# One recurrence step: gates and tanh of the cell held in PSUM, and the input gate activated on its own

## The reference, cut to what matters

```
def step(carry, xs):
    h, c = carry
    i_t = sigmoid(xi_t + h @ V_i)
    g_t = tanh(xg_t + h @ V_c)
    o_t = sigmoid(xo_t + h @ V_o)
    c_new = h * c + i_t * g_t
    h_new = o_t * tanh(c_new)
```

## Time and profile before

| | |
|---|---|
| median of three runs | 982.26 us |
| the profiled execution, its own time | 980.65 us |
| its span, first to last instruction | 978.9 us |
| mean granted TensorE clock | 0.755 of full speed |
| busy in the span: PE, DVE, ACT, POOL | 768.5, 552.2, 554.3, 369.5 us |
| first and last start of L470 | 145.7 us, 567.3 us |

### The profile page before, as it was taken

The page is one execution under the profiler, slowest core; times in us unless marked ns, Lnnn a source line. Parts: engine busy times, 40 slices in busy tenths (PEclk is TensorE's granted clock), DMA queues, the critical chain, the costliest instruction groups (busy, mean ns, idle before and its releaser), DMA issues.

```text
span 978.9 us, 18102 instructions
## 1 busy us (share of the span) xinstructions
PE 768.5 (79%) x6224; PEld 572.3 (58%) x6224; DVE 552.2 (56%) x1558; ACT 554.3 (57%) x1579; POOL 369.5 (38%) x296
## 2 busy tenths in 40 slices
PE   6899986666666666666666468999869999899996
PEld 3578875555555555555555445778736666466663
DVE  3788744555355355333333337887466676567665
ACT  3677743333355355333333336767558888688884
POOL 0877710000000000000000008777158888588884
PEclk9999985555555555555555559999879999899999
DMA  9600000000001100000000000000000010100001
GB/s 224 164 2 1 3 1 1 1 1 1 0 1 76 76 1 1 1 1 1 1 1 0 1 0 1 2 1 2 1 1 2 1 77 2 78 2 1 2 1 23
DMA packets 5861, 18.54 MB, mean 19 GB/s; under 512 B 1093, under 2 KB 2822, under 8 KB 5254
## 3 DMA queue, kind: packets, MB, share of 16 engines
q1 hardware_dynamic: 5478, 17.21, 6.0%
q10 hardware_dynamic: 288, 0.13, 0.1%
HBM read 9.47 MB, written 0.52 MB: 10 GB/s over the span
## 4 chain that ended last, share of the span: by engine, by line
PE 36%; POOL 21%; DVE 15%; ACT 12%; issue 12%; DVEq 1%; POOLq 1%; DMA 0%; SPq 0%; ACTq 0%
POOL zw L829 21%; PE bank L470 10%; PE bank L472 6%; DVE bank L1068 6%; PE bank L339 5%; ACT scan_io L724 5%; PE bank L356 5%; ACT tcell L728 5%; PE bank L304 5%; DVE hr L1072 4%; DVE hid L904 2%; PE bank L277 1%; PE bank L326 1%; PE bank L272 1%; PE bank L369 1%
## 5 line engine op out<-in xcount | busy, mean ns | idle before, releaser
L789 POOL TENSOR_TENSOR st<-tent,tentx 128x768 f32<-128x768 f32 x96 | 150.8, 1604 | 510.5 <-DVE tentx L897 500.0
L829 POOL TENSOR_TENSOR zw<-hid,zw 128x512 f16<-128x512 f32 x176 | 203.9, 1159 | 49.3 <-ACT zw L756 36.0
L470 PE MATMUL bank<-hr,lv 64*64 64x8 f32 x512 | 97.2, 262 | 151.1 <-DVE hr L1072 151.1
L470 PEld LDWEIGHTS bank<-hr,lv 64*64 64x64 f32 x512 | 73.0, 202 | 197.7 <-DVE hr L1072 197.6
L1171 DVE SCALAR_TENSOR_TENSOR hid<-bank,wsc,st 128x512 f32<-128x512 f32 x176 | 132.0, 750 | 75.7 <-ACT st L760 70.3
L724 ACT ACTIVATE scan_io<-bank 64x16 f32<-64x16 f32 x256 | 47.6, 186 | 216.6 <-PE bank L472 216.4
L510 PE MATMUL bank<-st,wh 128*128 128x512 f16 x352 | 136.8, 389 | 11.9 <-POOL st L822 5.4
L760 ACT ACTIVATE st<-bank,wsc 128x512 f32<-128x512 f32 x176 | 121.0, 687 | 40.1 <-PE bank L511 22.4
L1068 DVE TENSOR_TENSOR_SCAN bank<-scan_io 64x24 f32<-64x24 f32 x256 | 53.0, 207 | 157.8 <-ACT scan_io L724 157.7
L511 PE MATMUL bank<-st,wl 128*128 128x512 f16 x352 | 136.5, 388 | 0.0
L525 PEld LDWEIGHTS bank<-w2p,zw 128*128 128x128 f16 x1408 | 97.0, 98 | 45.4 <-POOL zw L829 4.1
(11 more groups left out here) (145 smaller groups left out, 1130.0 us busy)
## 6 DMA issues: line engine op xcount, KB each, us to landing
w13s<-w SPq DMA_DIRECT2D x8, 704.0 KB, 15.8
w2f<-w SPq DMA_DIRECT2D x4, 384.0 KB, 25.6
w13s<-wh SPq DMA_DIRECT2D x2, 704.0 KB, 3.4
w13s<-wl SPq DMA_DIRECT2D x2, 704.0 KB, 4.5
wh<-w13s SPq DMA_DIRECT2D x2, 704.0 KB, 3.8
wl<-w13s SPq DMA_DIRECT2D x2, 704.0 KB, 5.1
w2f<-w2p SPq DMA_DIRECT2D x2, 384.0 KB, 4.8
w2p<-w2f SPq DMA_DIRECT2D x2, 384.0 KB, 5.7
```

What stands on the lines that cost most here:

```text
L470: nc.tensor.matmul(both[:, 0, t, :], lv[:, C:2 * C], prev, start=False, stop=True, skip_group_check=True)
L789: nc.gpsimd.tensor_tensor(st[p][:, t, k:k + KG, :].rearrange("p k (y x) -> p k y x", x=16), ty, tx, ALU.mult)\
L829: nc.gpsimd.tensor_tensor(hl[:, u % MR, :], hid[:, u % MR, :], hh[:, u % MR, :], ALU.subtract)\
```

## The change

```diff
-        scan_io = sb("scan_io", [C, 2 * B * 3 + 8])
-        cell = bank[7][0:C, 0:B * 3].rearrange("p (b k) -> p b k", k=3)
...
-        tcell = sb("tcell", [C, B])
+        scan_add = sb("scan_add", [C, B, 3])
+        cell = bank[0][0:C, 32:32 + B * 3].rearrange("p (b k) -> p b k", k=3)
+        gates = bank[0][0:C, 0:B * 3]
+        gate_in = gates.rearrange("p (b k) -> p k b", k=3)
+        kept = scan_add[:, :, 2]
+        tcell = bank[0][0:C, 64:64 + B]
+        def gate_banks(r, t):
+            q = r % 2
+            return [bk[0:C, lo:lo + 128].rearrange("p (b t) -> p t b", t=W)[:, t, :]
+                    for bk, lo in ((bank[3 + q], 0), (bank[5 - 4 * q], 0), (bank[6 + q], 0))]
# PE, gates_x and the step
-                                     start=(gate != 1), stop=False, skip_group_check=True)
+                                     start=True, stop=False, skip_group_check=True)
-                nc.tensor.matmul(both[:, 0, t, :], lv[:, C:2 * C], prev, start=False, stop=True,
-                                 skip_group_check=True)
-                nc.tensor.matmul(both[:, 1, t, :], lv[:, 0:C], prev, start=False, stop=True,
+                nc.tensor.matmul(gi, lv[:, C:2 * C], prev, start=False, stop=True,
+                                 skip_group_check=True).then_inc(s("l_i"), 1)
+                nc.tensor.matmul(gg, lv[:, 0:C], prev, start=False, stop=True,
                                  skip_group_check=True).then_inc(s("l_gi"), 1)
# ACT
-            act.wait_ge(s("l_init"), 3)
+            act.wait_ge(s("l_zero"), 1)
+                if n > 0:
+                    act.wait_ge(s("l_hc"), n)
+                act.wait_ge(s("l_i"), n + 1)
+                nc.scalar.activation(gate_in[:, 1, :], gi, ACT.Tanh).then_inc(s("l_iact"), 1)
                 act.wait_ge(s("l_gi"), n + 1)
-                nc.scalar.activation(scan_ig, both, ACT.Tanh).then_inc(s("l_act"), 1)
+                nc.scalar.activation(gate_in[:, 2, :], gg, ACT.Tanh).then_inc(s("l_act"), 1)
# DVE
+            dve.wait_ge(s("n1_xn"), 1)
+            nc.vector.memset(gates, 0.0).then_inc(s("l_zero"), 1)
+                dve.wait_ge(s("l_iact"), n + 1)
                 dve.wait_ge(s("l_act"), n + 1)
                 nc.vector.tensor_tensor_scan(cell[:, :, :].rearrange("p b k -> p (b k)"),
-                                             scan_mul, scan_add, 0.0, ALU.mult, ALU.add).then_inc(s("l_c"), 1)
+                                             gates, scan_add[:, :, :].rearrange("p b k -> p (b k)"), 0.0, ALU.mult, ALU.add).then_inc(s("l_c"), 1)
-                    nc.vector.scalar_tensor_tensor(out=scan_hc, in0=hr[:, n % (2 * W), :], scalar=0.5,
+                    nc.vector.scalar_tensor_tensor(out=kept, in0=hr[:, n % (2 * W), :], scalar=0.5,
```

More of the change, by code:

```diff
@@ L198, in build @@
                   "w_part", "w_max", "w_tr", "w_pow", "w_bc", "w_scale", "w_fac", "w_high", "w_split", "w_stored", "l_scaled",
-                  "l_gi", "l_o", "l_act", "l_oact", "l_c", "l_tc", "l_h", "l_hc", "l_up", "l_res", "l_init",
+                  "l_i", "l_gi", "l_o", "l_iact", "l_act", "l_oact", "l_c", "l_tc", "l_h", "l_hc", "l_up", "l_res", "l_init", "l_zero",
                   "m_w0", "m_w1", "m_high", "m_scaled", "m_parts", "m_log", "m_max", "m_exp", "m_sm", "m_ge",
@@ L429, in gates_x @@
                 lo = (C, 0, 2 * C)[gate]
-                bk, col = (bank[5 + q], 0) if gate == 2 else (bank[3 + q], gate * 128)
+                bk, col = ((bank[3 + q], 0), (bank[5 - 4 * q], 0), (bank[6 + q], 0))[gate]
                 if part == 0:
                     nc.tensor.matmul(bk[0:C, col:col + 128], lb[:, lo:lo + C], ones[:, :],
-                                     start=(gate != 1), stop=False, skip_group_check=True)
+                                     start=True, stop=False, skip_group_check=True)
                 else:
@@ L452, in largest_weights @@
                 for k in range(2):
-                    nc.tensor.transpose(bank[0][0:1, k * 128:k * 128 + 128], wmax[:, k:k + 1], ident[:, :])\
+                    nc.tensor.transpose(bank[2][0:1, k * 128:k * 128 + 128], wmax[:, k:k + 1], ident[:, :])\
                         .then_inc(s("w_tr"), 1)
@@ L457, in spread_scales @@
                 pe.wait_ge(s("w_pow"), 3)
-                nc.tensor.matmul(bank[1][:, 0:2], ones[:, :], wpow[:, 2, :], start=True, stop=True)\
+                nc.tensor.matmul(bank[2][:, 256:258], ones[:, :], wpow[:, 2, :], start=True, stop=True)\
                     .then_inc(s("w_bc"), 1)
@@ L467, in _ @@
                 prev = hr[:, (n - 1) % (2 * W), :]
-                both = bank[3 + r % 2][0:C, 0:256].rearrange("p (k b t) -> p k t b", k=2, t=W)
-                go = bank[5 + r % 2][0:C, 0:128].rearrange("p (b t) -> p t b", t=W)[:, t, :]
-                nc.tensor.matmul(both[:, 0, t, :], lv[:, C:2 * C], prev, start=False, stop=True,
-                                 skip_group_check=True)
-                nc.tensor.matmul(both[:, 1, t, :], lv[:, 0:C], prev, start=False, stop=True,
+                gi, gg, go = gate_banks(r, t)
+                nc.tensor.matmul(gi, lv[:, C:2 * C], prev, start=False, stop=True,
+                                 skip_group_check=True).then_inc(s("l_i"), 1)
+                nc.tensor.matmul(gg, lv[:, 0:C], prev, start=False, stop=True,
                                  skip_group_check=True).then_inc(s("l_gi"), 1)
@@ L716, in lift @@
                                      ACT.Copy, scale=0.5).then_inc(s("l_up"), 1)
-            act.wait_ge(s("l_init"), 3)
+            act.wait_ge(s("l_zero"), 1)
             for n in range(STEPS):
                 r, t = n // W, n % W
-                both = bank[3 + r % 2][0:C, 0:256].rearrange("p (k b t) -> p k t b", k=2, t=W)[:, :, t, :]
-                go = bank[5 + r % 2][0:C, 0:128].rearrange("p (b t) -> p t b", t=W)[:, t, :]
+                gi, gg, go = gate_banks(r, t)
+                if n > 0:
+                    act.wait_ge(s("l_hc"), n)
+                act.wait_ge(s("l_i"), n + 1)
+                nc.scalar.activation(gate_in[:, 1, :], gi, ACT.Tanh).then_inc(s("l_iact"), 1)
                 act.wait_ge(s("l_gi"), n + 1)
-                nc.scalar.activation(scan_ig, both, ACT.Tanh).then_inc(s("l_act"), 1)
+                nc.scalar.activation(gate_in[:, 2, :], gg, ACT.Tanh).then_inc(s("l_act"), 1)
                 act.wait_ge(s("l_o"), n + 1)
@@ L953, in _ @@
             nc.vector.memset(ones[:, :], 1.0).then_inc(s("l_init"), 1)
-            nc.vector.memset(scan_io[:, :], 0.0).then_inc(s("l_init"), 1)
+            nc.vector.memset(scan_add[:, :, :], 1.0).then_inc(s("l_init"), 1)
             dve.wait_ge(s("l_init"), 2)
-            nc.vector.memset(scan_one, 1.0).then_inc(s("l_init"), 1)
+            nc.vector.memset(kept, 0.0).then_inc(s("l_init"), 1)
             nc.vector.memset(hr[:, 2 * W - 1, :], 0.0).then_inc(s("l_h"), 1)
@@ L1011, in scales @@
                 elif k == 4:
-                    power("w", wpow, bank[0], WTOP)
+                    power("w", wpow, bank[2], WTOP)
                 elif k == 9:
                     dve.wait_ge(s("w_bc"), 1)
-                    nc.vector.tensor_copy(wsc[:, 2:4], bank[1][:, 0:2]).then_inc(s("w_scale"), 1)
+                    nc.vector.tensor_copy(wsc[:, 2:4], bank[2][:, 256:258]).then_inc(s("w_scale"), 1)
                 elif k == 10:
-                    nc.vector.reciprocal(wsc[:, 0:2], bank[1][:, 0:2]).then_inc(s("w_scale"), 1)
+                    nc.vector.reciprocal(wsc[:, 0:2], bank[2][:, 256:258]).then_inc(s("w_scale"), 1)
                 elif k == 11:
```

## The result

Five runs of each kernel gave a median of 974.30 us (971.44 to 975.79) after and 982.26 us (980.42 to 983.58) before: a ratio of 0.9919, 95% interval 0.9897 to 0.9941. The change makes the kernel faster by 8.0 us, 0.8%, where 15 us had been forecast. The time lies inside the stated range of 956 to 979 us, but outside the 956 to 973 of the forecast's own terms. The profiled execution took 974.3 us with a span of 972.5 (before 980.65 and 978.9).

A forecast was written before the change was run, and what follows sets the result against it. The prediction took a chain of waits through the recurrence, 255 intervals, as the bound, no engine. 15 + 2 x 22 = 59 ns a step gave 15.0 us, 982.3 to 967.2 us; range 956 to 979.

The forecast's parts named there:

- the forecast's own terms: Recurrence step: shorter candidate tanh plus two PSUM writes each shorter by 11 to 44 ns; 956 to 973 us, chance 0.78.
- The candidate's tanh: L724 in the recurrence step: shrinking from 64x16 to 64x8 saves 15 ns a step on the path.
- the activations that write PSUM: Candidate's activation and L728: writing PSUM instead of SBUF saves 22 ns each, 44 ns a step; lower end 0, upper 44 each.
- The 22: Nanoseconds saved per activation writing PSUM, the middle of 11 and 34 ns from rows reading PSUM against SBUF.
- DVE's PSUM operands: Scan's multipliers and tcell in L1072, read from PSUM: cost 0, bounds -2 to +50 ns at each place.
- Rival B: Scan and L1072: a PSUM operand costs DVE more than ACT gains; at the bound +10.5 us, 993; chance 0.06.
- The input gate's own tanh: New ACT activation after L470: covered while the candidate waits for L472, 0.09 us to spare; value 0, bounds 0 and +20 ns.
- DVE's third wait: l_iact joins l_act ahead of the scan, met earlier by more than 0.1 us; value 0, bounds 0 and +40 ns.
- Rival C: New waits on the path: tanhs not overlapping (+20 ns) and a late l_iact instruction (+40); time stays at 982; chance 0.04.
- rival A: Activations on the path: writing PSUM gains nothing, only the 15 ns remain, 3.8 us, 978.5; chance 0.10.
- The sum: Recurrence: 15 + 2 x 22 = 59 ns a step, 15.0 us over 255 steps; 967.2 us expected, 1.585 us a step.
- D: PE clock rises to 2.4 GHz for part of the recurrence, shortening L470 and L472; 26 us on top, 941; chance 0.02.

The follow-up runs named there:

- the kernel of 932.79 us: The changed kernel with DVE's waits reordered so that the scan carries l_act and L1079 carries l_tc: 932.79 us, ratio 0.9500.

## Why the prediction was right in its sign and half wrong in its size

**What bounds the kernel.** Right. It is a chain of waits, and PE, the busiest engine of the stage, is busy for 270.6 of 411.9 us. In each experiment the time followed the step: 255 times what the step gained gives the measured gain within 1.5 us, but for the kernel of 932.79 us, where it gives 53 and 49 were measured.

**The candidate's tanh, and the activations that write PSUM.** Right in sum, 149 ns forecast for both and 147 measured for both, with some luck in the parts. At L724's place the smaller size was worth 11 ns, not 15 (186 to 175 with the gates in SBUF), and PSUM 28, not 22; at L728's place PSUM was worth 24. The 22 was the middle between two pairs of rows (11 and 34 ns) that differ in their source, not their destination, and also in operation, type or partitions. Nothing ahead of the run said that the middle was the right value. For the page of the Trainium skill that the prediction names ("Perfetto Trace Analysis", "Optimizing Scalar/DVE Operations"), its 42 ns less for ScalarE has the right sign and is above the 24 and 28 measured for a PSUM destination and the 31 for a PSUM source. The section calls its figures engine-busy times, and the lengths here are those of the profile's records, so the two are not quite the same quantity.

**DVE's PSUM operands.** Right, and slightly better than the lower bound of -2 ns: the scan 207 and 207, the output multiply 155 against 159. Rival B is out. The VectorE half of that section of the Trainium skill, 65 ns more in PSUM, does not show in the records of these reads. Only the output showed a price, of 8 or 9 ns.

**The input gate's own tanh.** Right in an ordinary step: covered, with 0.07 to spare where 0.09 had been worked out, and the spacing of 0.08 that was read from the earlier trace rows is seen again where ACT had stalled. What the prediction did not have is that stall itself. It made five steps 0.18 to 0.20 us late, 4 ns a step in the mean, inside the bound of 20.

**DVE's third wait: the step that failed.** "I take 0, bounds 0 and +40 ns." It was +30 (0.02 to 0.05), and that is the term that was mis-sized. The prediction asked whether `l_iact` is met earlier than `l_act`, which it is, by 0.15, and whether the check would be one more instruction, which it is not. What the runs showed in its place: the wait that comes last stands in a sequencer instruction on the path, and that instruction takes longer when it has two semaphores to check, even when one was met before. 255 x 0.03 = 7.7 us; the kernel without it is at 966.5, where 967 had been forecast for the change. Rival C had this price, but only together with two tanhs that don't overlap (20 + 40 ns, 0.04); no chance was given to the wait alone. The stated range held the result only because it had been widened for rival A, which is not what happened.

**The sum.** With the traces' own numbers, in an ordinary step: -39 (L724's place) - 24 - 4 + 30 = -37 ns, where the step went from 1.646 to 1.607 us, 39 less; the 2 between them is rounding (the hand-over to the scan by the records grew by 28 or 29). The mean step fell by 37, because late steps cost 2 ns a step more than before. Forecast were 59: the activations gave 63 and L1079 another 4, and the wait took 30 back. The 1.585 us a step that the prediction gives should read 1.581 (1.64 less 0.059) for an ordinary step, or 1.594 for the mean. In us: 9.5 saved in the chain, 8.0 in the medians of the runs, 6.4 in the one profiled span; the stages around the recurrence spread over 557 to 562 us, which covers the distance between the first and the last.

**The clock.** It stayed at 0.50 in the whole recurrence. D is out.

**What the prediction did not see.** It read the 0.10 between ACT and DVE correctly as 0.03, 0.02 and 0.04 around a sequencer instruction and took it as given. It is not: it depends on which of two waits the instruction itself carries, and the order of two source lines decides that. Two such pairs of lines were worth 36 us in the kernel before, more than four times the change.

## What to carry to other kernels

In a loop bound by a chain of short instructions, look in the chain of waits for a sequencer's row (DVEq, ACTq): it means that the wait that ends last is not carried by the instruction. Put the wait that comes last first in the source, so that the instruction carries it and the others are checked in idle time, if they are met early enough. Split an instruction so as to start half of it earlier only after counting the semaphores that the consumer then checks on the path; give the two halves one count where they run in order on one engine.

## What the runs showed of the hardware that I had not expected

- A late wait in a sequencer instruction ahead of a DVE instruction costs about 70 ns against a carried one: by the chain, the hand-over from ACT is 0.09 us with it and 0.02 without, at both places of the step (together 1.653 to 1.511 us).
- A second semaphore in that instruction costs 30 ns more when it is on the path (0.02 to 0.05 us on DVE), and nothing when it is off it (1.438 and 1.437 us a step). ACT had no such instruction with two semaphores.
- A tanh on 64x8 takes 171 ns from PSUM to SBUF, 178 from SBUF to PSUM, and 147 within PSUM. Where it writes every third element of SBUF (`gates`) it takes 175, and 147 with the same layout in PSUM. So the destination is worth 24 or 28 ns at 8 elements, and 33 for the joined 16.
- For DVE a PSUM source was no dearer than an SBUF one: 155 against 159 ns and 157 against 162 for a 64x8 multiply, 207 against 207 or 208 for the scan. A PSUM output cost the scan 8 or 9 ns.
- ACT stood idle for 0.32 to 0.34 us between a sequencer instruction and its activation in five of 256 steps. DVE has such stalls too, of 0.40 or 0.41 us where 0.04 is usual, in five steps of the kernel before and in three of the changed one. No run here says why.
